# The last group's layer-1 probabilities turned by TensorE instead of a DMA, its last gate on VectorE, and the last three groups in a new order

## The reference, cut to what matters

```python
# block 0, per batch element (q = x, k = v = ctx)
attn = einsum(qh, kh) + rel_bias[idx]
p = softmax(attn / 8);  out = (p @ vh) @ fc_w.T + fc_b
x = q + out;  x = x + gelu(ln(x) @ W1.T + b1) @ W2.T + b2
# block 1 (query = x, key = value = ctx)
scores = where(window, q @ k.T / 4, NEG);  probs = softmax(scores)
attn = (probs @ v) @ Wo + bo
gate = silu(concat([attn, query]) @ Wg + bg)
out = attn * gate + query * (1 - gate)
x_hat = out * rsqrt(mean(out * out) + eps) * rms_w
return x_hat - mean(x_hat, axis=tokens)
```

## Time and profile before

| what | value |
|---|---|
| median of the runs | 1823.62 us |
| the profiled execution | 1823.93 us |
| its span | 1822.1 us |
| TensorE busy | 1790.1 us, 98% |
| ScalarE busy | 1546.5 us, 85% |
| VectorE busy | 1467.8 us, 81% |
| GpSimd busy | 1274.7 us, 70% |
| mean granted TensorE clock | 0.999 |

### The profile page before, as it was taken

How to read it: one execution, slowest core, us unless ns; L and a number is a source line. 1 busy time by engine, 2 the same in 40 slices (tenths; PEclk the granted TensorE clock), 3 DMA queues, 4 the chain that set the end, 5 groups by cost and what they waited for, 6 DMA issues and landing times.

```text
span 1822.1 us, 55343 instructions
## 1 busy us (share of the span) xinstructions
PE 1790.1 (98%) x18768; PEld 1659.9 (91%) x18768; DVE 1467.8 (81%) x6755; ACT 1546.5 (85%) x5586; POOL 1274.7 (70%) x1324
## 2 busy tenths in 40 slices
PE   7999999999999999999999999999999999999998
PEld 5989999999999999999999999999999989999987
DVE  6878888887788888788887788888888877878864
ACT  5688889888889888889888889888889888898874
POOL 3556777767777767777766777776777776776754
PEclk9999999999999999999999999999999999999999
DMA  6434454444454444454444444444454444544442
GB/s 231 123 100 117 115 135 122 119 116 115 120 134 118 124 113 115 121 133 117 126 115 110 124 128 119 126 116 111 125 131 114 123 119 110 132 115 121 100 98 59
DMA packets 238058, 219.10 MB, mean 120 GB/s; under 512 B 48848, under 2 KB 220240, under 8 KB 237776
## 3 DMA queue, kind: packets, MB, share of 16 engines
q1 hardware_dynamic: 237776, 215.57, 46.0%
HBM read 71.29 MB, written 9.96 MB: 45 GB/s over the span
## 4 chain that ended last, share of the span: by engine, by line
PE 78%; SPq 6%; DMA 5%; DVE 5%; POOL 2%; ACT 2%; issue 2%; POOLq 0%; DVEq 0%; ACTq 0%
PE bank L624 9%; PE bank L626 9%; PE bank L625 9%; PE bank L638 7%; PE bank L642 7%; PE bank L639 7%; PE bank L811 6%; PE bank L798 6%; SPq L257 5%; PE bank L923 4%; PE bank L936 3%; PE bank L630 3%; DMA soft<-turned 3%; PE bank L631 2%; PE bank L634 2%
## 5 line engine op out<-in xcount | busy, mean ns | idle before, releaser
L2525 ACT ACTIVATE soft<-soft,row_min 128x128 f32<-128x128 f32 x1024 | 398.2, 393 | 47.3 <-DVE row_min L1651 46.8
L2605 ACT ACTIVATE soft<-soft,row_min 128x128 f32<-128x128 f32 x1024 | 396.1, 390 | 42.3 <-DVE row_min L1759 42.3
L3054 POOL TENSOR_TENSOR soft<-soft,inv_sum 128x512 f32<-128x512 f32 x256 | 268.3, 1054 | 172.2 <-DVE inv_sum L1659 135.4
L247 DVE STREAM_TRANSPOSE turned<-soft 128x512 f32<-128x512 f32 x512 | 344.7, 691 | 30.1 <-DMA soft<-turned 18.8
L3063 POOL TENSOR_TENSOR soft<-soft,inv_sum 128x512 f32<-128x512 f32 x256 | 264.7, 1046 | 109.5 <-DVE inv_sum L1768 109.4
L1651 DVE CUSTOM_DVE_ANT_0 soft<-bank,relb 128x128 f32<-128x128 f32 x1024 | 231.0, 282 | 39.3 <-PE bank L798 39.1
L1759 DVE CUSTOM_DVE_ANT_0 soft<-bank,winb 128x128 f32<-128x128 f32 x1024 | 224.0, 281 | 36.8 <-PE bank L923 35.3
L2525 ACT ACTIVATION_READ_ACCUMULATOR soft<-soft,row_min 128x1 f32 x1024 | 195.2, 191 | 0.0
L2605 ACT ACTIVATION_READ_ACCUMULATOR soft<-soft,row_min 128x1 f32 x1024 | 193.2, 189 | 0.0
L624 PE MATMUL bank<-wv,cT 128*128 128x256 f32 x512 | 144.0, 281 | 0.0
L625 PE MATMUL bank<-wv,cT 128*128 128x256 f32 x512 | 143.7, 281 | 0.0
(11 more groups left out here) (249 smaller groups left out, 6426.1 us busy)
## 6 DMA issues: line engine op xcount, KB each, us to landing
soft<-turned SPq DMA_DIRECT2D x1024, 128.0 KB, 2.8
tokens<-stats_by_row SPq DMA_DIRECT2D x63, 256.0 KB, 3.4
tokens<-in_x SPq DMA_DIRECT2D x32, 256.0 KB, 3.0
raw<-in_x_t SPq DMA_DIRECT2D x32, 256.0 KB, 3.9
x<-in_x SPq DMA_DIRECT2D x32, 256.0 KB, 2.8
out<-gate SPq DMA_DIRECT2D x63, 128.0 KB, 2.6
tokens<-in_ctx SPq DMA_DIRECT2D x31, 256.0 KB, 3.0
raw<-in_ctx_t SPq DMA_DIRECT2D x31, 256.0 KB, 3.1
```

The lines of the kernel that those rows point to most:

```text
L247: return eng.transpose(turned[:, slot, :, s % 2, :, :].rearrange("p j h b -> p h j b"), soft[:, s, :, :].rearrange("p h (j a) -> p h j a", ...
L2525: last = act.activation(soft[:, s, h, :], soft[:, s, h, :], ACT.Exp, bias=row_min[:, s, h:h + 1], scale=-1.0, accum_out=row_sum[:, s, h:h ...
L2605: last = act.activation(soft[:, s, h, :], soft[:, s, h, :], ACT.Exp, bias=row_min[:, s, h:h + 1], scale=-1.0, accum_out=row_sum[:, s, h:h ...
L3054: pool.tensor_tensor(soft[:, slot0(g, m), :, :], soft[:, slot0(g, m), :, :], inv_sum[:, slot0(g, m), :].unsqueeze(2).broadcast_to([P, QUAD ...
```

## The change

In the last group alone, `turn1` and `spread1` of block 1 go. `norm1` now writes its product to `turned`, with the keys of a head put in order (a step of four elements between neighbours in the writing, none in the reading). A new step `turn_p` transposes the four heads of a unit on TensorE to a bank, and a new step `place1` copies the bank to the places in `soft` that `spread1` filled; `pv1` waits for it. For the very last batch element, `times_z`, `times_gate`, `plus_x` and `x_hat_lo` go from GpSimd to VectorE. All five programs of the epilogue are in a new order, with new banks; the numbers of filler matmuls change from 25, 60 and 26 to 24, 21 + 3 and 24.

```diff
+        def in_key_order(u):
+            return turned[:, 1 + u // 2, :, :, :, :].rearrange("p j m h b -> p (j m h b)")[
+                :, u % 2 * BANK:(u % 2 + 1) * BANK].rearrange("p (h n) -> p h n", h=QUAD)
...
+            def turn_p(g, b, u, bank, *drains):
+                freed(till, *drains)
+                till.wait_ge("norm1", unit1(g, b, u) + 1)
+                for h in range(QUAD):
+                    last = pe.transpose(bank[:, h * SEQ:(h + 1) * SEQ], in_key_order(u)[:, h, :], ident[:])
+                last.then_inc(sem["turn_p"], 1)
...
                     till.wait_ge("kv_out", g + 1)
-                till.wait_ge(f"spread1_{n}", 16 * NB * (GROUP * g + b + 1))
+                if g == NG - 1:
+                    till.wait_ge("place1", NU1 * b + 2 * n + 2)
+                else:
+                    till.wait_ge(f"spread1_{n}", 16 * NB * (GROUP * g + b + 1))
...
+            def place1(g, b, u, bank):
+                till.wait_ge("turn_p", NU1 * b + u + 1)
+                till.wait_ge("norm1", unit1(g, b, u | 1) + 1)
+                dve.tensor_copy(pair_of_slots(u // 2 if beside(g, b) else 2 + u // 2)[:, :, u % 2, :, :],
+                                bank[:].rearrange("p (h i b) -> p i h b", h=QUAD, i=NB)).then_inc(sem["place1"], 1)
...
+            def times_gate_last(g, b):
+                till.wait_ge("minus_x", GROUP * g + b + 1)
+                till.wait_ge("times_z", GROUP * g + b + 1)
+                till.wait_ge("times_gate", GROUP * g + b)
+                dve.tensor_tensor(att_of(g, b), att_of(g, b), gate_of(g, b), ALU.mult).then_inc(sem["times_gate"], 1)
...
+                if g == NG - 1:
+                    if b == 0:
+                        till.wait_ge(f"spread1_{u // 2}", 16 * NB * GROUP * g)
+                    else:
+                        till.wait_ge("turn_p", u + 1)
+                    pool.tensor_tensor(in_key_order(u).rearrange("p h (a j) -> p h j a", j=NB),
+                                       soft[:, s, :, :].rearrange("p h (j a) -> p h j a", j=NB),
+                                       inv_sum[:, s, :].unsqueeze(2).unsqueeze(3).broadcast_to([P, QUAD, NB, BLOCK]),
+                                       ALU.mult).then_inc(sem["norm1"], 1)
+                    return
...
-            kv(NG - 1, banks[7], ("ag", 2 * NG - 4))
+            kv(NG - 1, banks[4], ("y_out", 2 * NG - 4))
```

More of the change, by code:

```diff
@@ new lines, in tensor_program @@
+            scores1(NG - 5, 1, (banks[2], banks[6], banks[7], banks[5]), (("min0", 8 * NG - 21),), (("min0", 8 * NG - 20),), (("k_out", 4 * NG - 9),), (("kv_turn", NG - 2),))
+            pv1(NG - 5, 0, 0, banks[3], ("v_out", 4 * NG - 11))
+            pv1(NG - 5, 0, 1, banks[3])
+            center_out(NG - 6, 1, banks[0], ("x1", NG - 3))
+            proj_k(NG - 3, 3, banks[4], ("q_out", 4 * NG - 9))
+            out_mm(NG - 5, 0, banks[1], ("q_out", 4 * NG - 8))
+            pv(NG - 3, 0, banks[2], ("min1", 8 * NG - 35))
@@ new lines, in tensor_program @@
+            pv1(NG - 4, 0, 0, banks[3], ("o_lo", 4 * NG - 8))
+            scores(NG - 2, 2, (banks[7], banks[6]), (("v_out", 4 * NG - 7),), (("min0", 8 * NG - 12),))
+            kv(NG - 2, banks[4], ("x1", NG - 2))
+            pv1(NG - 4, 0, 1, banks[3])
+            center_out(NG - 5, 1, banks[0], ("min1", 8 * NG - 27))
+            proj_k(NG - 2, 3, banks[2], ("min1", 8 * NG - 26))
+            out_mm(NG - 4, 0, banks[4], ("kv_turn", NG - 1))
+            out_mm_lo(NG - 4, 0, banks[4])
+            proj_q(NG - 2, 3, banks[3], ("o1_lo", 2 * NG - 7))
@@ new lines, in tensor_program @@
+            proj_q(NG - 1, 0, banks[4], ("hid_out", 4 * NG - 8))
+            proj_q_lo(NG - 1, banks[4])
+            mlp_out(NG - 3, 1, 0, banks[6])
+            mlp_out(NG - 3, 1, 1, banks[6])
+            center_out(NG - 4, 0, banks[7], ("min0", 8 * NG - 9))
+            mlp_out_lo(NG - 3, 1, 0, banks[6])
+            mlp_out_lo(NG - 3, 1, 1, banks[6])
+            out_mm(NG - 4, 1, banks[2], ("min0", 8 * NG - 8))
+            out_mm_lo(NG - 4, 1, banks[2])
+            turn_x2(NG - 3, banks[1], ("o1_lo", 2 * NG - 6))
@@ new lines, in tensor_program @@
+            mlp_out_lo(NG - 2, 1, 1, banks[2])
+            out_mm(NG - 3, 1, banks[3], ("o_lo", 4 * NG - 2))
+            turn_x2(NG - 2, banks[5], ("min0", 8 * NG - 1))
+            out_mm_lo(NG - 3, 1, banks[3])
+            fc_lo(NG - 1, 0, banks[6])
+            proj_q1(NG - 2, banks[7], ("y_out", 2 * NG - 5))
+            proj_q1_lo(NG - 2, banks[7])
+            pv(NG - 1, 2, banks[4], ("o1_lo", 2 * NG - 4))
+            scores1(NG - 2, 0, (banks[0], banks[2], banks[1], banks[5]), (("min0", 8 * NG),), (("x2", NG - 1),), (("v_out", 4 * NG - 1),), (("x2_lo", NG - 1),))
@@ new lines, in tensor_program @@
+            keep_busy(banks[3], 24, ("v_out", 4 * NG))
+            turn_h(NG - 1, banks[3], ("v_out", 4 * NG))
+            mlp_in(NG - 1, 0, banks[5], ("min1", 8 * NG - 12))
+            mlp_in_lo(NG - 1, banks[5])
+            mlp_in(NG - 1, 1, banks[7], ("o_lo", 4 * NG))
+            center_out(NG - 3, 1, banks[4], ("min1", 8 * NG - 11))
+            pv1(NG - 2, 0, 0, banks[0], ("min1", 8 * NG - 10))
+            pv1(NG - 2, 0, 1, banks[0])
+            out_mm(NG - 2, 0, banks[6], ("x1", NG))
@@ new lines, in tensor_program @@
+            mlp_out(NG - 1, 1, 0, banks[3])
+            mlp_out(NG - 1, 1, 1, banks[3])
+            mlp_out_lo(NG - 1, 1, 0, banks[3])
+            center_out(NG - 2, 0, banks[7], ("hid_out", 4 * NG - 2))
+            mlp_out_lo(NG - 1, 1, 1, banks[3])
+            out_mm(NG - 2, 1, banks[0], ("o1_lo", 2 * NG - 3))
+            turn_x2(NG - 1, banks[6], ("ag", 2 * NG - 3))
+            proj_q1(NG - 1, banks[2], ("hid_out", 4 * NG - 1))
+            proj_q1_lo(NG - 1, banks[2])
+            out_mm_lo(NG - 2, 1, banks[0])
@@ new lines, in tensor_program @@
+            scores1(NG - 1, 0, (banks[1], banks[4], banks[7], banks[5]), (("hid_out", 4 * NG),), (("kv_turn", NG),), (("y_out", 2 * NG - 3),), (("o1_lo", 2 * NG - 2),))
+            scores1(NG - 1, 1, (banks[3], banks[6], banks[2], banks[0]), (("x2", NG),), (("x2_lo", NG),), (("q1_out", NG),), (("ag", 2 * NG - 2),))
+            keep_busy(banks[1], 21, ("min1", 8 * NG - 7))
+            turn_p(NG - 1, 0, 0, banks[1], ("min1", 8 * NG - 7))
+            turn_p(NG - 1, 0, 1, banks[4], ("min1", 8 * NG - 6))
@@ L1429, in tensor_program @@
+            out_mm(NG - 1, 0, banks[4], ("place1", 2))
+            turn_p(NG - 1, 1, 3, banks[7], ("place1", 3))
+            out_mm_lo(NG - 1, 0, banks[4])
+            pv1(NG - 1, 1, 0, banks[3], ("place1", 4))
+            pv1(NG - 1, 1, 1, banks[3])
+            out_mm(NG - 1, 1, banks[6], ("y_out", 2 * NG - 2))
             out_mm_lo(NG - 1, 1, banks[6])
-            keep_busy(banks[1], 26, ("min1", 8 * NG - 2))
-            center_out(NG - 1, 0, banks[1], ("min1", 8 * NG - 2))
-            center_out(NG - 1, 1, banks[3], ("min1", 8 * NG - 1))
+            keep_busy(banks[5], 24, ("o1_lo", 2 * NG - 1))
@@ L1434, in vector_program @@
+            center_out(NG - 1, 0, banks[5], ("o1_lo", 2 * NG - 1))
+            center_out(NG - 1, 1, banks[2], ("place1", 5))
         def vector_program(dve):
@@ L3442, in gpsimd_program @@
             norm1(NG - 1, 1, 3)
-            x_hat_lo(NG - 2, 1)
             minus_x(NG - 1, 0)
```

1063 lines of the change are left out of this document (509 added, 554 removed).

## The result

After the change the time was 1814.72 us (median of 4 runs, 1813.73 to 1815.47) against 1823.3 before (4 runs, 1822.97 to 1825.36). Of the later runs of before, one took 2896.63 us at a mean clock of 0.56 and is left out everywhere. The ratio is 0.9948, with a 95% interval of 0.9933 to 0.9963, so 6.7 to 12.2 us faster, 9.5 at the middle. I had forecast 1817.6 with a range from 1814.5 to 1822.0, so faster by 6.

What follows compares the result with a forecast made beforehand. TensorE was taken to bound the bulk and a chain of waits the epilogue. Gains of 0.8, 4.4 and 1.6 less 0.8 for the clock made 6.0 us, from 1823.62 to 1817.6; range 1814.5 to 1822.0.

Steps and rivals of the forecast that it cites:

- the bulk taken at nothing: Ahead of the epilogue's end, where TensorE had no idle time, reordering the same work was to gain 0.
- a loss by the clock: In the tail, half a dip of TensorE's clock at a gap ahead of center_out was to lose 0.8 us.
- Up to F: Up to F, the last group's first exponential: 0.8 us gained, from hidden kv (0.36) and x2_hi beginning 0.45 earlier.
- Block 1 of the last group: From the first exponential to the last sum: 4.4 us gained, the sum beginning at F+20.33 and not F+24.70.
- So the DMAs did not set the end; the order did: In the old tail, pv1 of the second element was held by TensorE's order, not by the 16 DMAs.
- The last gate: From the last sum's end to y_out's end: 1.6 us gained, 8.26 before; bounds 0.6 to 2.1.
- The wait beside GpSimd: In the last gate, steps moved to VectorE wait up to 0.7 us for GpSimd's plus_x; 0.4 was taken.
- Rival A: TensorE's clock stays low through the tail, losing 4.5 us and not 0.8: 1821.3 us; chance 0.12.
- B: In the last group, norm1 with stepped writing is dear: 1821 us at 1.6 each, up to 1828; chance 0.09.
- C: The new order stalls TensorE in the bulk: 3 us give 1820.6, 8 us give 1825; chance 0.10.
- D: The last group's keys come late and delay its first exponential: 1819 to 1821 us; chance 0.06.
- the signs of being wrong: TensorE idle above 1 us (1600 to 1750), norm1 above 1.2, half clock over 3 us after F+9, scores1 awaiting keys.

Runs made afterwards that it cites:

- name-only kernel: Also spelled n_names: the kernel before with only two more names in its list of semaphores; ratio to before 0.9988 (0.9977 to 0.9999).
- the gate's run: The changed kernel with times_z, times_gate, plus_x and x_hat_lo of the last batch element back on GpSimd; ratio to before 0.9960.
- s_split: The changed kernel with one pv in the loop moved behind one mlp_out, making one more run of small matmuls a round; ratio to before 1.0004.
- s_delay: The changed kernel with one mlp_out in the loop moved ahead of two pv1 and the pv, small matmuls kept together; ratio to before 1.0133.
- the second profile of before: The kernel before run and profiled once more with no edit; ratio to before 0.9996 (0.9982 to 1.0011).
- h_old_tail: The changed kernel's new order up to the last group's scores, then the old tail (turn1, spread1, gate on GpSimd); ratio to before 0.9997.
- c_no_filler: The changed kernel without the 21 and 3 filler matmuls between the last scores and the first turn_p; ratio to before 0.9962.
- the second measurement: The changed kernel measured again with no edit: median 1817.56 us of 10 runs, ratio to before 0.9962.
- o_order_only: The kernel before, DMAs and turn1 kept, with the norm of the last batch element but one moved earlier, plus two semaphore names; ratio to before 1.0011.

## Why the prediction was right, and where it was wrong

The forecast was too small. Two of its steps failed, the bulk taken at nothing and a loss by the clock, and two terms were mis-sized.

**Up to F: forecast 0.8, found 2.5.** This is a step that failed: "I take the bulk at nothing: the same work in a new order with no idle time before can't gain". To F it is 208.99 to 210.68 us in five profiles with the old order (mean 209.8), and 206.88 to 207.92 in nine with the new (mean 207.3). From the filler's start to F it is 0.6 of that (33.5 became 32.9; forecast 0.45 for x2_hi, with kv hidden as worked out). From the loop's end to the filler it is 1.9, where I had 0.36 for kv. This is no idle time saved: with the waits taken off, the stretch is 175.6 to 176.2 us in the five and 173.9 to 174.2 in the nine, 1.8 less on the mean. The distances between matmuls show where. 0.36 is the kv, as forecast. 0.3 is turn_x2 of NG-3: in the old order it stands right behind pv1, and out_mm comes 0.65 us after its start where it else is 0.35. 0.2 is turn_h of NG-3, whose successor comes 0.53 us after its start in the old order, where that is scores, and 0.35 in the new.

```profile
1678.08 1.08 PE L936 MATMUL bank<-soft,vpad 128*32 128x128 f32 x32
1679.09 0.66 PE L648 MATMUL bank<-ident,x 128*128 128x128 f32 x4
1679.74 0.47 PE L638 MATMUL bank<-wog,o1T 128*128 128x512 f32 x1
```

(This is the name-only kernel; in the changed kernel's second profile turn_x2 starts at 1687.32 and its successor at 1687.67.) The other 0.9 lies in small amounts at other changes from one kind of matmul to another; two runs of small matmuls fewer are about 0.4 of it by the price above. All this is read from distances, and no run tried these places apart. (The working has two misreadings that change no sum: from 1700 to 1750 it is VectorE that has 40 us and ScalarE 44, the 46 are TensorE's weight loads; and turn_x2 held out_mm from 1778.29 to 1778.67, so for 0.38 us and not 0.63.)

**Block 1 of the last group: forecast 4.4, found 4.38 between the two profiles, but 3.1 as a rule.** Each marker of the new tail held: the last exponential ended at F+13.14 (13.1), turn_p took 0.60 to 0.66 (0.63), place1 0.60 from start to start where nothing held it (0.62), out_mm of the first element began at F+13.55 (13.55), and the last sum at F+20.32 (20.33), the same within 0.02 us in all six new tails with all their filler and their order (the four of the table and the gate's run, s_split and s_delay). Mis-sized was the old side: F+24.70 held the dip, and without one the old tail takes 23.43 and 23.48. The step "So the DMAs did not set the end; the order did" was wrong as well. It holds only for the one execution with the dip. Without it the last DMA's landing released the last pv1 (F+19.78 and F+19.83), 0.2 to 0.3 us behind the order, and with the order alone mended the DMAs take over at once. It is right that the new tail takes both away.

**The last gate: forecast 1.6, found 1.33**, in every profile within 0.01. The wait beside GpSimd fell on times_z (0.83 for 0.42, beside GpSimd's plus_x at 1803.89), as forecast at 0.4. The trace agrees there with the lock of the Trainium skill (SBUF — State Buffer, Who interferes with whom). times_gate and plus_x met no GpSimd work and took 0.42. Term by term: the three moved steps gave 0.65 (0.7), mean_sq 0.36 (0.4). x_hat_lo gave 0.13 and not 0.3, since it waited for GpSimd's x_hat_lo of the first element, which took 0.99 for 0.73 beside VectorE's x_hat. rrms_ took 0.81 for 0.55, beside the other x_hat, and lost 0.27 that no term had; x_hat took 0.48 for 0.94 and gained 0.45 that no term had either. The 0.15 for hops didn't come.

```profile
1807.58 0.48 DVE L1865 SCALAR_TENSOR_TENSOR normed<-normed,moments,rows 128x256 f32<-128x256 f32 x1 [0.44 <-POOL moments L3239]
1808.75 0.43 DVE L1851 TENSOR_TENSOR xT<-normed,xT 128x256 fp32r<-128x256 f32 x1 [0.69 <-POOL o1T L3232]
```

**The clock: forecast a loss of 0.8, found none.** This is the other step that failed. I took half a dip for a gap "as large" ahead of center_out. The waits there came to 0.52 and 0.36 us and not 1.1, and no new tail with its filler shows a dip. And such a gap alone doesn't decide: the name-only kernel, the second profile of before and h_old_tail have the same waits as before up to there (1.09 or 1.10 ahead of center_out, 0.58 ahead of out_mm) and no dip at that point. This is the name-only kernel at F+17.3, where before it stood at 0.50:

```profile
1799.00:1800.00 1.00, 1.00 (x8) 0.87 (x7) 0.23 (x1) 0.00 (x0) 0.00 (x0) 1.00 0.82 208
```

So the dip of before was there in one of four executions with the same waits, and cost 1.2 to 1.3 us; what decides it no run here shows. Rival A didn't come: with transposes among filler and matmuls the clock stayed at 1.00. Only without the filler did a part of it, at 1.85 us. The Trainium skill (TensorE: Matmul & The Clock Gate, Part 4) has it that the full clock does not engage for transposes; with 24 fillers among them this trace shows none of that, and without them (c_no_filler) it can't be told apart from the idle time.

**Rivals B, C and D.** B didn't come: norm1 took 1.12 to 1.17, and one 1.38 beside VectorE's x_hat. C: TensorE waited 1.1 us in the profile after between the loop's end and the filler, at pv1 and pv, and 0 to 0.5 in the others with the new order. So two of the signs of being wrong were met by a little (1 us of idle time, 1.2 for a norm1), and neither cost the forecast its gain. D: the keys were hidden.

**The sum and the range.** The change is worth 2.5 + 3.1 + 1.3 = 6.9 us, and 1.2 more where before has its dip; the second measurement has 6.9 too. My 6.0 was low by 1.7 in the first term and by 0.8 for the clock, and high by 1.3 in the second and 0.3 in the third. The rest up to the 9.5 of the first measurement is the scatter of the loop. My range was built from the change's terms only, with three runs of before that lay 2.4 us apart. The later ones spread from 1819 to 1830. The lower end of the range had no room for that. By the second measurement alone the forecast would have stood inside its range, and that would have been luck: the two steps that failed and the two that were mis-sized nearly cancel (1.7 and 0.8 against 1.3 and 0.3).

## What to carry to other kernels

Cut both traces at events that the change doesn't touch before reading any difference: here a third of it lay in identical code. An engine that lists no idle time can still be ordered better: here each change of a matmul's shape of rows and columns cost it about a tenth of a microsecond; count the seams. A piece of a tail that is timed once may hold an event that the next execution doesn't have: ask a second profile before it becomes a term. And before calling a cause ruled out, ask how far behind the other one it stands: here the DMAs were 0.2 to 0.3 us behind the order.

## What the runs showed of the hardware that I had not expected

One more run of small matmuls between large ones cost 0.19 us a round (s_split), with no idle time listed. Four transposes of 128x128 right behind a pv1 hold the next matmul for 0.65 us, and for 0.35 behind a large one (0.53 if scores follow). With the same waits to 0.01 us the clock fell to half in one execution's tail and not in three others (before, against its second profile, n_names and h_old_tail). The DMAs of one and the same loop land so differently that pv1's waits there sum to 3.6 us in one profile (o_order_only) and to 10.1 in another (h_old_tail). Where VectorE's x_hat and a GpSimd step overlapped in the changed kernel, it was GpSimd's, begun 0.07 to 0.08 us later, that took longer (0.81 for 0.55, 0.99 for 0.73).
